# A graph layer on one core: the first stage's turned rows kept in the accumulator and stored by ScalarE at the stage's end

## The reference, cut to what matters

```python
xn = _layernorm(x, axis=-1)
x = x + gnn(xn, edges, edge_attr) + mix(xn)      # two graph attention layers; one linear attention over all nodes
x = x + ffn(_layernorm(x, axis=-1))              # 6 experts, each node goes to its best 2

# one graph attention layer (8 heads of 32)
xp = (x @ W).reshape(-1, Hh, C)
alpha = leaky_relu(a_src[src] + a_dst[dst] + a_edge, 0.2)
alpha = segment_softmax(alpha, dst)              # over the edges that end in a node
out = segment_sum(xp[src] * alpha[:, :, None], dst) + bias

# mix: q, k, v from xn; squares of centred q and k, scaled; kv = k2' v; t2 = q2 kv / sqrt(N)
return (v + t2) @ W_out + b_out
```

## Time and profile before

| | us |
|---|---|
| median of 3 runs | 3738.2 |
| lowest, highest | 3726.09, 3741.85 |
| profiled execution | 3723.76 |
| its span | 3722.0 |
| first stage, up to ScalarE's last copy | about 111 |
| first instructions of edge stage 0 | 118.6 |

### The profile page before, as it was taken

How to read it: one execution, slowest core, us unless ns; L and a number is a source line. 1 busy time by engine, 2 the same in 40 slices (tenths; PEclk the granted TensorE clock), 3 DMA queues, 4 the chain that set the end, 5 groups by cost and what they waited for, 6 DMA issues and landing times. The chain is left out here.

```text
span 3722.0 us, 60054 instructions
## 1 busy us (share of the span) xinstructions
PE 2531.6 (68%) x15613; PEld 2146.8 (58%) x15614; DVE 2126.3 (57%) x6066; ACT 1171.6 (31%) x4747; POOL 2014.2 (54%) x2269
## 2 busy tenths in 40 slices
PE   6467667666676767683666666666666666859898
PEld 4355555555565556562555555555555555638787
DVE  6355555555555655652555555555555556766565
ACT  3133333333333333351222222222222224522222
POOL 3555555555555555535555555555555554726665
PEclk8677777778777777896777777777777777869999
DMA  9544444444444444314444444444444443545433
GB/s 255 153 119 119 116 122 117 120 117 128 114 126 121 123 120 126 109 64 117 134 121 136 125 129 134 125 135 126 138 126 133 131 124 87 165 134 160 151 114 96
DMA packets 282397, 475.71 MB, mean 128 GB/s; under 512 B 69124, under 2 KB 191644, under 8 KB 282116
## 3 DMA queue, kind: packets, MB, share of 16 engines
q0 software_dynamic: 96912, 288.68, 28.2%
q1 hardware_dynamic: 120884, 137.12, 12.2%
q10 hardware_dynamic: 64320, 46.56, 4.0%
HBM read 398.47 MB, written 75.78 MB: 127 GB/s over the span
## 5 line engine op out<-in xcount | busy, mean ns | idle before, releaser
L707 POOL DMA_INDIRECT e_rows<-table,e_idx x1664 | 1578.9, 949 | 1305.0 <-DVE e_msg L747 950.3
L1087 PE MATMUL e_ps_sum<-e_hot,e_msg 128*128 128x129 f32 x6656 | 1358.4, 351 | 871.5 <-ACT parts L943 477.3
L1087 PEld LDWEIGHTS e_ps_sum<-e_hot,e_msg 128*128 128x128 f32 x6656 | 1138.1, 247 | 1028.1 <-issue 604.9
L942 ACT ACTIVATE acc<-e_ps_sum 128x256 f32 x1664 | 641.2, 385 | 1931.3 <-PE e_ps_sum L1087 814.4
L726 DVE TENSOR_TENSOR e_hot<-e_ps_pr,rel 128x512 f32<-128x512 f32 x416 | 285.5, 686 | 829.0 <-PE e_ps_sum L1087 406.7
L747 DVE TENSOR_TENSOR e_msg<-e_rows,e_ps_pr 128x256 f32<-128x256 f32 x1664 | 654.7, 414 | 40.0 <-remote 5.3
L943 ACT ACTIVATE parts<-e_ps_sum 128x4 f32<-128x4 f32 x1664 | 281.0, 169 | 0.0
L1069 PE MATMUL e_ps_al<-e_dst_score,e_hotT 128*128 x3328 | 217.6, 179 | 52.1 <-issue 44.4
L1069 PEld LDWEIGHTS e_ps_al<-e_dst_score,e_hotT 128*128 128x128 bf16 x3328 | 199.3, 103 | 81.4 <-issue 51.2
L737 DVE TENSOR_SCALAR e_hotT<-e_relb,pcolf 128x512 bf16<-128x512 bf16 x416 | 144.6, 348 | 38.9 <-issue 23.9
L2281 ACT ACTIVATE x_h<-x,eb 128x128 f32<-128x128 f32 x216 | 67.7, 364 | 273.6 <-PE x L2355 227.5
(11 more groups left out here) (370 smaller groups left out, 3400.3 us busy)
## 6 DMA issues: line engine op xcount, KB each, us to landing
e_relb<-rel_rows SPq DMA_DIRECT2D x104, 512.0 KB
e_rows<-table,e_idx POOLq DMA_INDIRECT x1664
e_eattr<-in_edge_b SPq DMA_DIRECT2D x104, 128.0 KB
e_xT<-turned_x ACTq DMA_DIRECT2D x100, 128.0 KB
e_xr<-in_x ACTq DMA_DIRECT2D x100, 128.0 KB
node<-l_row SPq DMA_DIRECT2D x25, 512.0 KB, 3.1
table<-t_row SPq DMA_DIRECT2D x25, 276.0 KB
table<-j_row SPq DMA_DIRECT2D x25, 276.0 KB, 2.4
```

What stands on the lines that cost most here:

```text
L707: nc.gpsimd.indirect_dma_start(out=rows[q][:, k, :], out_offset=None, in_=table[0:NP], in_offset=bass.IndirectOffsetOnAxis(ap=idx[:, q, k: ...
L942: nc.scalar.activation(acc[:, :, bass.ds(at[k], P)], ps_sum[(k + q) % 3][:, :, 0:P], ACT.Copy).then_inc(s["window"], 1)
L1087: op = nc.tensor.matmul(ps_sum[(k + q) % 3][:, a, 0:WIN], msg[:, k % RM, a * P:a * P + P], hot[:, q, k, :], start=(a == 0), stop=True, ski ...
```

## The change

The copy of the turned chunk goes to `acc` instead of `xnT`: chunk n has its own 256 columns there, so no buffer has to come free, and the semaphores `xo0` and `xo1` go. SP no longer stores the turned chunks. ScalarE issues the 25 stores itself, one after another, when its last row copy is done. They count on a new semaphore `turned_out`, which lives beyond the block. In edge stage 0 ScalarE waits for all 25 behind its first exponential, since its window copies overwrite `acc`, and only then loads block 0. In layer 1 the load of block 0 stays where it was. VectorE's zeros in the last columns of `acc` go as well.

```diff
+        turned_out = sem("turned_out", top)
         first(nc, sb, pb, sem, locals())
@@ first
+    xnT = v["acc"]
-        xnT = tmp("xnT", [P, 2, 2, CH])
-                 "split", "xo0", "xo1", *(f"out{q}" for q in range(RR)), ...
+                 "split", *(f"out{q}" for q in range(RR)), ...
@@ SP
                 if n + 4 < NCH:
                     fetch(n + 4)
-                sp.wait_ge(s["copied"], n + 1)
-                sp.dma_start(turned_x[n], xnT[:, n % 2]).then_inc(s[f"xo{n % 2}"], 16)
                 if n >= 3:
                     store(n - 3)
...
-            for q in range(2):
-                sp.wait_ge(s[f"xo{q}"], 16 * (NCH // 2 + (q == 0)))
@@ VectorE
-                nc.vector.memset(v["acc"][:, :, N:NP], 0.0)
@@ ScalarE
                 act.wait_ge(s["turned"], n + 1)
-                if n >= 2:
-                    act.wait_ge(s[f"xo{n % 2}"], 16 * (n // 2))
-                nc.scalar.activation(xnT[:, n % 2], turn[n % 2][:].rearrange("p (a n) -> p a n", a=2), ACT.Copy
+                nc.scalar.activation(xnT[:, :, n * CH:n * CH + CH], turn[n % 2][:].rearrange("p (a n) -> p a n", a=2), ACT.Copy
                                      ).then_inc(s["copied"], 1)
...
             rows(NCH - 1)
+            act.wait_ge(s["copied"], NCH)
+            for n in range(NCH):
+                act.dma_start(turned_x[n], xnT[:, :, n * CH:n * CH + CH]).then_inc(v["turned_out"], 16)
@@ edges, ScalarE
-            fetch_block(0, 0, 0)
             if layer == 1:
+                fetch_block(0, 0, 0)
                 act.wait_ge(s["kxT"], 1)
                 ...
             exps(0, 0)
+            if layer == 0:
+                act.wait_ge(v["turned_out"], 16 * NCH)
+                fetch_block(0, 0, 0)
             step(0, 0, 0)
```

More of the change, by code:

```diff
@@ L221, in first @@
         names = ("w", "x0", "x1", "x2", "x3", "iota", "mv", "rstd", "xn", "turned", "copied", "rectified", "row", "rowc",
-                 "split", "xo0", "xo1", *(f"out{q}" for q in range(RR)), "edge_in", "dst_in", "marks_in", "att_in", "cols_in", "kq_in", "v_in", "src_in",
+                 "split", *(f"out{q}" for q in range(RR)), "edge_in", "dst_in", "marks_in", "att_in", "cols_in", "kq_in", "v_in", "src_in",
                  "rel", "rel_t", "rel_c", "marks", "bvb", "wv_t", "wv_c", "product", "stored")
```

## The result

The changed kernel takes 3749.98 us (median of 8 runs, 3738.03 to 3759.39), the kernel before 3738.59 us (8 runs, 3726.09 to 3741.85). The ratio is 1.0038, 95% interval [1.0019, 1.0056]: 7 to 21 us slower. The time lies in the forecast range (3725 to 3757), and the change moved it the way that was forecast. But the loss is 11 us, not 4.

A forecast was written before the change was run, and what follows sets the result against it. The first stage was taken as bound by transfers from 57 to 92 us, with the DMA engines full. Handover +10.8 minus first stage 6.4 gave +4.4 us, edge stage's start 0; forecast 3740 us, range 3725 to 3757.

The forecast's parts named there:

- First stage, -6.4 us: First stage: with the turned stores out of SP's queue it ends 6.4 us earlier; ends 3 and 19.4.
- The step on chunk 5: First stage, 18.1 to 20.92 us: x of chunk 5 is loaded earlier, so VectorE waits 1.8 us less.
- The other steps (3.0 + 1.3 + 0.3): First stage: four stores fewer ahead of x 3.0 us, `marks` starting earlier 1.3, VectorE's memset of `acc` gone 0.3.
- ScalarE's 19.2 us: First stage, 60 to 92 us: ScalarE's waits for turned stores, not added because VectorE waits for x there too.
- The second rival: First stage gives back far more, 15 of VectorE's 19.4 us of waits; sum -4.2 us, 3734; chance 0.15.
- Handover, +10.8 us: First stage's end to edge stage: 15 us of ScalarE's issues plus 3.3, minus 7.5 before; ends +5.3 and +18.9.
- the 3.3 us behind the last issue: Handover: from the last engine's arrival to the edge stage, 2.9 us clearing semaphores plus 0.4 for the barrier.
- 7 can be outstanding: Handover: ScalarE is free after 18 of 25 stores have moved, 13.5 us plus about 1.5 shared with table stores.
- The rival in which the queue takes everything in 9.5 us: Handover: all 25 issues go out unheld, handover +5.3 us, sum -1.1, time 3735 to 3737; chance 0.2.
- Edge stage's start, 0: Start of edge stage 0: the wait for 25 stores and later fetch of block 0 are hidden by GpSimd's gathers, cost 0.
- The slower rival: Edge stage's start: ScalarE held to the end (+18.9), leftover stores hold GpSimd's gathers 4 us; sum +20, 3758; chance 0.15.
- the last rival: Edge stage: no store moves beside it, since all are issued before the barrier; nearly the forecast itself, no chance given.

The follow-up runs named there:

- e1: Changed kernel, but ScalarE issues the 25 stores behind the barrier, at the start of edge stage 0; ratio to the kernel before 0.9991 [0.9965, 1.0016].
- e9: Changed kernel with each store laid out as 128 pieces of 2 KB instead of 256 of 1 KB; one run, 20.5 us from last row copy to edge stage.
- e2: Changed kernel, but ScalarE issues all 25 stores inside the loop, none at its end; ratio to the kernel before 0.9979 [0.9954, 1.0005].
- e6: As e1, but ScalarE first waits until the table pieces have landed; ratio to the kernel before 0.9992 [0.9969, 1.0015].
- e4: Changed kernel, but stores of chunks 0 to 12 issued inside the loop, 12 left for the end; one run, 12.9 us from last row copy to edge stage.
- e12: Kernel before with marks stored once and the second group's gathers held until the first group's scores are done; ratio to the kernel before 0.9972 [0.9953, 0.9991].

## Why the prediction was right in kind and short in size

- **Which stage, and what bounds it:** right. `marks` and x fill the queue from 57 to 92 us; with `marks` stored once the waits for x are gone and 13.5 us with them.
- **First stage, -6.4 us:** the sign is right, the size is 4.1 (mean of four stages against two, standard error 2, so 6.4 is not excluded). The step on chunk 5 gave nothing: x came in time, but VectorE then waited 2.4 us for GpSimd's `rstd`, which stands in order behind a row split, and was at the same place at 62.7 us. That was 1.8 of the 6.4. The other steps (3.0 + 1.3 + 0.3) agree with the 4.1 in sum; none of them was measured by itself. The waits for the turned stores became waits for the table stores, so ScalarE's 19.2 us were rightly not added. The second rival (15 us given back) is out.
- **Handover, +10.8 us: the term that was mis-sized.** It measured +15.5. The time of a store, 0.75 us, was right (0.78), and so were the 3.3 us behind the last issue (3.5). What failed is "7 can be outstanding": ScalarE is let go with 2.8 stores outstanding, 2.2 us before the data end. The estimate of 1700 to 2000 packets was read from SP's queue in a stretch with `marks` in it, and did not carry over to ScalarE's queue here. It isn't wrong everywhere: in e1, beside the table pieces, 6.8 were outstanding. What decides between the two stays open, and e9 shows that it isn't a number of pieces. With 3 for 7 the sum gives 22 x 0.77 + 1.5 = 18.4 us of issues against 19.3 measured. The rival in which the queue takes everything in 9.5 us is out. Its price was too low as well: 0.34 us is an issue of 128 pieces on SP's queue, and ScalarE's issue of a store of 256 pieces took 0.52 us in e2 even where nothing held it, which would be 14 us for 25. The section of the Trainium skill that this rival named, "Anatomy of one DMA — SWDGE (gpsimd) path" in "DMA: Bandwidth & Descriptors", describes DMAs issued from GpSimd. These stores went through a queue that the trace lists as hardware_dynamic, so the runs don't test its rule; they show only that it doesn't forecast ScalarE's issues.
- **Edge stage's start, 0:** nearly right. The first scores are 46.1 and 46.3 us after it instead of 45.4 and 45.8, 0.6 us. The wait for the 25 stores was over long before, and the fetch of block 0 lay in idle time.
- **Sum:** 15.5 - 4.1 + 0.6 = 12.0 us, against 15.2 at the first window in the first pair of profiles, 12.9 in the means of both pairs, and 11.4 between the medians. That 3750 lies in the range owes something to its width: the range reaches 17 us above the forecast.
- **The slower rival** had two halves. ScalarE was held nearly to the end, as it said (+15.5 of its +18.9). Its leftover stores beside the gathers never came, since the stores were through 1.4 us before the stage began, as the last rival had it. e1 and e6, which put the stores there, had their first scores 2 to 4 us further from the stage's start, but with GpSimd's pitch unchanged.

## What to carry to other kernels

A store "begun" at a stage's end is a store paid at its end if the barrier waits for the issue: in the changed kernel the issuing engine was let go only 3 before the last, so count bytes over bandwidth, not issues. Before moving traffic out of a full queue, ask which transfer sets its pace: here it was 3.4 MB of short rows that differ in nothing but a repeated index, and leaving 7 of 8 out gained more than any place for the 6.5 MB beside them. And look for the next wait in line: three of the waits removed here (the turned stores, the load of chunk 5, the first scores) came back nearly whole one instruction later.

## What the runs showed of the hardware

- The DMA queues of ScalarE and SP moved the same number of packets side by side, whatever the sizes: 1010 of 1 KB beside 1008 of 48 B in 4 us (e1), so that TensorE could use the small one's 300 KB only 32.9 us after the stage's start instead of 12.8.
- An issue is held by more than its own size: SP's load behind the table pieces was held 6.25 us in the changed kernel and 23.6 in e1. And how far an engine runs ahead of its stores is not one number: 2.8 stores of 256 KB (changed, e4), 2.9 (e9, with pieces twice as large), 3.4 (e6), 6.8 (e1).
- A store of 256 KB took 0.34 us to issue in 128 pieces (before, on SP's queue; e9's first, on ScalarE's) and 0.52 us in 256 pieces (e2, on ScalarE's), where nothing held it.
- Taking 256 KB stores out of a queue full of 516 B rows lowered its rate (234 to 197 GB/s) rather than its time.
- The same kernel took 3722 to 3767 us in four groups of runs and 2982 in one. In the former, VectorE's first scores, and in e12 ScalarE's first window, went on only 3.9 to 7.1 us after GpSimd's uninterrupted row of indirect DMAs had ended, though TensorE's part of the work had been done many us before (e1 is apart: there TensorE's own scores were late); in the group at 2982 (e9) the first scores came 23.0 us after the stage's start, with 14 gathers of the row still to go. TensorE's granted clock was 0.50 in this stretch in both, so it doesn't explain this difference; over the whole span its mean was 0.78 against 0.88 to 0.89. Two groups on the same chip fell on either side (2982 and 3722 us), so it is not the chip. What sets it stays open.
